# Self attention's tail in another order on TensorE, VectorE and ScalarE, and a routed unit's wait put later

## The chip, the cores and the metric

One Trainium2 chip, one core of it. The metric is the device time of one execution in microseconds (us), as the median of several runs. TensorE does matrix products and transposes into PSUM (eight banks), VectorE and ScalarE read PSUM and write SBUF, GpSimd works from SBUF to SBUF, and the SyncE queue issues most transfers. Engines run on their own and meet at semaphores.

## The reference

One layer: cross attention, self attention and a mixture of experts, each added to x. 1024 tokens of 256 numbers, in float32; what matters here is self attention's end and the experts.

```python
def _L0_attn_ref(x, Wq, Wk, Wv, Wo):          # 16 sequences of 64, 16 heads of 16
    q, k, v = ...                              # x @ Wq, x @ Wk, x @ Wv, by heads
    scores = jnp.einsum('bthd,bshd->bhts', q, k)
    scores = scores * mask                     # lower triangle; the rest becomes 0
    attn = jax.nn.softmax(scores / T ** 0.5, axis=-1)
    return jnp.einsum('bhts,bshd->bthd', attn, v).reshape(B, T, H * Dh) @ Wo

def _L0_ffn_ref(x, w_router, wg, wu, wd, sg, su, sd):   # 8 experts, 2 per token, 2 shared
    scores = jax.nn.sigmoid(logits)
    topk_w, topk_i = jax.lax.top_k(scores, TOPK)
    topk_w = topk_w / jnp.sum(topk_w, axis=-1, keepdims=True)
    ...                                        # silu(x wg) * (x wu), times wd, weighted
    out = out + jnp.einsum('tji,jhi->th', sgate * sup, sd)   # the shared experts

x = x + _L0_xattn_ref(_layernorm(x), ctx_2048, ...)
x = x + _L0_attn_ref(_layernorm(x), ...)
x = x + _L0_ffn_ref(_layernorm(x), ...)
```

## The kernel before

The tokens are worked in eight tiles of 128 (NT = 8). Each engine has its own program, written out in order; there is no scheduler, so the order of the code is the order of the work, and semaphores (`wait_ge`, `then_inc`) tie the engines together. An instruction that waits holds up everything behind it on its engine.

Self attention takes a tile through these steps: TensorE's scores into PSUM banks 0 and 1 (`b_scores`); VectorE masks them and takes each row's maximum (`b_maximum`, lines 672 and 676); GpSimd subtracts it (`b_subtract`, line 528); ScalarE takes the exponential (`b_exp`, line 1233); TensorE transposes the probabilities into banks 4 and 5 (`b_probs_T`); ScalarE copies them to SBUF (line 1241); TensorE multiplies by the values into banks 6 and 7 (`b_values`, line 1681); VectorE divides by the sums (`b_divide`, lines 829 and 835); TensorE transposes the result into bank 2 (`b_transposes`), ScalarE copies it (`b_OT_out`, line 1227), TensorE projects it (`b_project`, line 1689), and VectorE adds it to x and takes the mean and variance (`b_residual`, lines 573 to 578). The loop over tiles keeps three tiles in flight. The code around the change is what stands behind that loop: the last steps of tiles 5, 6 and 7 (NT - 3, NT - 2, NT - 1), mixed with the first steps of the experts.

These are: GpSimd's reciprocal root of the variance (`c_rstd`, line 532), VectorE's normalized rows in pairs of tiles (`c_norms`, line 870, into `xn3`, a part of `x_up`), TensorE's transposes of such a pair (`c_transposes(g)`, four of them into bank `CT_BANK[g]`), ScalarE's copy into `xT_all` (`c_xT_out`, line 1257), and the first shared expert's products over pairs of tiles: `shared_up(m)` (line 1725, into bank `UP_BANK[m]`: 0, 1, 3, 2 and on), ScalarE's silu (`gated`, line 1262), VectorE's product (`product`, line 880) and `shared_down` (line 1737). The router's products (`logits`, line 1757) need all eight tiles transposed. All transposes have line 1320. Line 1725's groups of eight in the trace are one `shared_up`: each float32 product counts twice.

Then 20 routed units run, each of 64 rows of one expert and 64 of another. `pair_a(u)` and `pair_b(u)` (line 1817) multiply the unit's transposed rows `xnT` by the gate and up weights into banks 0, 2 and 1, 3; `hidden_T(u)` transposes the hidden rows into banks 4 and 5; `pair_down(u)` (line 1841) multiplies by the down weights into bank 6. ScalarE copies a unit's rows in `routed_x` (line 1294); it must have the products of the unit ahead behind it, since there is one `xnT`. The shared expert's last sum of the first part (group 4, bank 5) is added to x by `shared_out` (line 973), which raises `added`. Second experts' rows come by transfers of 1280 KB (line 433).

Where a wait stands matters in a plain way: `pe.wait_ge(s, n)` stops TensorE until semaphore `s` has reached `n`.

Of the kernel before, what the change touches and what calls it, by code (L numbers as in the profile page):

```python
# [25 lines left out]
NT = T // P  # L26
# [24 lines left out]
MF = GF * IC  # L51
MN = len(PAIRS) * IC
UP_BANK = [(0, 1, 3, 2)[m % 4] for m in range(MF)] + [(7, 0, 2)[m % 3] for m in range(MN - MF)]
CT_BANK = (1, 3, 6, 7)
Y_BANK = [(5, 5), (4, 4), (5, 5), (4, 4), (5, 5), (1, 1), (3, 3), (4, 5)]


# [35 lines left out]
def build(nc, dram):  # L93
    with ExitStack() as ctx:
# [468 lines left out]
        def _(dve):  # L563
# [114 lines left out]
            def b_maximum(i):  # L678
                dve.wait_ge(bs_ps, i + 1)
                after(dve, bp_done, i)  # L680
                b_masked().then_inc(bs_used, 1)
                dve.wait_ge(bs_used, i + 1)
                b_top().then_inc(bmax, 1)
# [156 lines left out]
            def b_residual(i, link_, b=5):  # L840
                dve.wait_ge(bproj_ps, i + 1)
                join(i, link_, b, x3_done)
# [37 lines left out]
                dve.tensor_tensor(hidT_ring[m % 4], sil_ring[m % 2], ps[:, UP_BANK[m], D:2 * D], ALU.mult).then_inc(up_hid, 1)  # L880

            b_residual(NT - 4, link)
            b_maximum(NT - 1)
            c_norms(0, 2, 1)
            b_divide(NT - 2, link)
            b_residual(NT - 3, link, 3)
            c_norms(2, 4, 1)
            b_divide(NT - 1, link)
            product(0)
            b_residual(NT - 2, link)  # L890
            c_norms(4, 6, 2)
            product(1)
            b_residual(NT - 1, link)
# [138 lines left out]
        def _(act):  # L1032
# [5 lines left out]
            def two(b):  # L1038
                return ps[:, b:b + 2, :].rearrange("p b (h t) -> p (b h) t", t=P)
# [190 lines left out]
            def b_exp(i):  # L1230
                act.wait_ge(bsub, i + 1)

                act.activation(pr[:], sc[:], ACT.Exp, scale=SSCALE).then_inc(bp_done, 1)

            def b_step(i, parity, ahead, next_, behind):
                if ahead:
                    b_xT_out(i + 2)
                if behind:
                    b_OT_out(i - 1)
                act.wait_ge(bpt_ps, i + 1)  # L1240
                act.copy(prT, two(4)).then_inc(bpt_done, 1)
                if ahead:
                    b_k_out(i + 2)
                if next_:
                    b_exp(i + 1)
                if ahead:
                    b_v_out(i + 2, parity)
# [15 lines left out]

            act.wait_ge(absorb_m, 4)
            act.wait_ge(zeroed, 16 * ZC)
            b_step(NT - 2, 0, False, True, True)
            c_xT_out(0)
            b_step(NT - 1, 1, False, False, True)
            gated(0)
            gated(1)  # L1270
# [47 lines left out]
        def _(pe):  # L1318
# [449 lines left out]
            pe.wait_ge(bs_used, NT)  # L1768
            c_transposes(0)
            b_transposes(None, NT - 2)  # L1770
            b_probs_T(NT - 1)
            pe.wait_ge(ws_in, 16)
            pe.wait_ge(c_xT, 1)
            shared_up(0)
            b_values(NT - 1, 1)
            b_project(NT - 2)
            shared_up(1)
            b_transposes(None, NT - 1)
            pe.wait_ge(x3_done, NT - 2)
            c_transposes(1)  # L1780
            pe.wait_ge(x3_done, NT - 1)
            b_project(NT - 1)
            c_transposes(2)
            pe.wait_ge(c_xT, 2)
            shared_up(2)
            c_transposes(3)
            pe.wait_ge(bot_done, NT)
            shared_up(3)
            pe.wait_ge(x3_done, NT)
            shared_down(0)  # L1790
            pe.wait_ge(moe_in, 16)
# [76 lines left out]
            ahead = pair_a(0, now, True)  # L1868
            slots_T(1)
            pair_b(0, now)  # L1870
            pe.wait_ge(added, GF)

            for u in range(NU - 1):
                pe.wait_ge(uxT, u + 2)
                pe.wait_ge(b_up_in[(u + 1) % 2], 16 * ((u + 1) // 2 + 1))
                later = pair_a(u + 1, ahead, u + 2 < NU)
                hidden_T(u)
                pair_b(u + 1, ahead)
                if u + 2 < NU:
                    slots_T(u + 2)  # L1880
                pair_down(u, now)
                now, ahead = ahead, later
# [100 lines left out]
```

## Time and profile before

| | |
|---|---|
| median of 3 runs | 513.69 us (513.13 to 515.97) |
| the profiled execution | 514.32 us |
| its span | 512.5 us |
| TensorE busy | 496.6 us, 97% of the span |
| VectorE, ScalarE, GpSimd busy | 247.4, 185.1, 67.6 us |
| the chain that ended last | TensorE 87%, VectorE 6%, issue 3% |
| granted TensorE clock | 1.0 throughout |
| self attention's tail | 229.6 to 252.5 us of the span |
| first routed unit | from 312.0 us |

A row of the trace gives the start, the length, the engine, the line, the operation and the tiles. "x8" is the count of instructions merged into the row. A bracket at the end says how long the engine had been idle before it and whose end released it. A group's length is counted to the modelled end of its last product, so the next group starts a little before the row ahead of it ends. `w_routed` is the name of a large store, in parts of which self attention keeps its scores, probabilities and results until the experts' weights are loaded there; `x_up` holds the normalized rows.

### The profile page before, as it was taken

The page shows a single profiled execution, that of the slowest core. Times are in us where ns is not written, and L with a number is a line of the kernel's source. Part 1 is how long each engine was busy: PE and PEld are TensorE (multiplying, and loading weights), DVE is VectorE, ACT ScalarE, POOL GpSimd, SP SyncE. Part 2 cuts the span into 40 slices and gives each one's busy share as a digit, 9 for nine tenths or more (in the row PEclk, how much of TensorE's full clock was granted, in tenths as well). Part 3 has the DMA queues.
Part 4 walks back from the last instruction along what each step waited for, and adds up shares of the span by engine and source line. Part 5 has one row for each costly group of instructions (what it writes and reads, how often), then busy time and mean ns, then how long its engine had stood idle before and what let it go on. Part 6 is the DMA issues. An engine that isn't in the chain of part 4 may idle for free.

```text
span 512.5 us, 10574 instructions
## 1 busy us (share of the span) xinstructions
PE 496.6 (97%) x3878; PEld 361.1 (70%) x3878; DVE 247.4 (48%) x547; ACT 185.1 (36%) x533; POOL 67.6 (13%) x74
## 2 busy tenths in 40 slices
PE   8799999999999999998999998999999999999997
PEld 7566876876887788886788885555555555556886
DVE  2585776776776678888552221212212222222334
ACT  2267566666667544444411111212212112111110
POOL 6200000000000122232006500000000000000650
PEclk9999999999999999999999999999999999999999
DMA  7830000002990019300704272687877878852341
GB/s 224 300 113 22 0 22 20 0 20 82 369 388 2 2 62 428 128 0 1 277 35 133 73 263 60 262 299 258 313 278 268 321 265 280 306 198 83 86 120 41
DMA packets 24887, 82.05 MB, mean 160 GB/s; under 512 B 2928, under 2 KB 16560, under 8 KB 20880
## 3 DMA queue, kind: packets, MB, share of 16 engines
q1 hardware_dynamic: 21824, 73.30, 39.6%
q0 software_dynamic: 1536, 4.20, 2.6%
q10 hardware_dynamic: 1488, 4.00, 2.1%
q8 instruction: 28, 0.46, 0.3%
q14 instruction: 11, 0.09, 0.1%
HBM read 73.10 MB, written 8.39 MB: 159 GB/s over the span
## 4 chain that ended last, share of the span: by engine, by line
PE 87%; DVE 6%; issue 3%; DMA 1%; ACT 1%; SPq 0%; POOL 0%; DVEq 0%; POOLq 0%
PE ps L1817 17%; PE ps L1725 13%; PE ps L1320 12%; PE ps L1841 9%; PE ps L1737 6%; PE ps L1399 5%; PE ps L1349 5%; PE ps L1368 5%; PE ps L1491 3%; PE ps L1387 3%; DMA w_shared<-in_w_uqk 1%; PE ps L1341 1%; PE ps L1501 1%; PE ps L1681 1%; PE ps L1364 1%
## 5 line engine op out<-in xcount | busy, mean ns | idle before, releaser
L1817 PE MATMUL ps<-w_routed,xnT 128*64 x320 | 93.8, 436 | 1.6 <-DVE x_sb L973 1.6
L1725 PE MATMUL ps<-xT_all,w_shared 128*128 128x256 f32 x320 | 75.6, 380 | 0.0
L1817 PEld LDWEIGHTS ps<-w_routed,xnT 128*64 128x64 f32 x320 | 42.0, 137 | 38.4 <-issue 27.2
L1725 PEld LDWEIGHTS ps<-xT_all,w_shared 128*128 128x128 f32 x320 | 60.3, 190 | 8.4 <-issue 0.4
L1097 ACT ACTIVATE w_routed<-ps,neg_top 128x128 f32<-128x128 f32 x128 | 45.1, 379 | 15.9 <-DVE neg_top L648 15.9
L1841 PE MATMUL ps<-w_routed,hidT 128*64 x200 | 47.4, 384 | 0.0
L1817 PE MATMUL ps<-w_shared,xnT 128*64 128x384 f32 (+1 forms) x160 | 46.9, 436 | 0.0
L1817 PE MATMUL ps<-x_up,xnT 128*64 128x384 f32 (+1 forms) x160 | 46.9, 436 | 0.0
L1320 PEld LDWEIGHTS ps<-consts_a,w_routed 128*128 128x128 f32 x336 | 37.2, 141 | 13.5 <-issue 10.4
L1289 ACT COPY hidT<-ps 128x384 f32<-128x384 f32 x20 | 9.6, 479 | 100.7 <-PE ps L1320 100.7
L1262 ACT ACTIVATE sil<-ps 128x256 f32<-128x256 f32 x40 | 15.4, 384 | 84.3 <-PE ps L1725 84.2
L1320 PE MATMUL ps<-consts_a,w_routed 128*128 128x128 f32 x336 | 44.3, 276 | 1.1 <-DVE w_routed L835 0.5
L1841 PEld LDWEIGHTS ps<-w_routed,hidT 128*64 128x64 f32 x200 | 25.8, 137 | 15.0 <-issue 3.3
L1368 PEld LDWEIGHTS ps<-hid,w_routed 128*128 128x128 f32 x256 | 33.6, 192 | 1.2
L967 DVE COPY hidT<-ps 128x256 f32<-128x256 f32 x20 | 8.5, 425 | 53.4 <-PE ps L1320 53.4
L1368 PE MATMUL ps<-hid,w_routed 128*128 128x128 f32 x256 | 33.7, 275 | 0.0
L558 POOL DMA_INDIRECT x_up<-y_slots,slot_i x8 | 8.0, 997 | 182.7 <-DVE hidT L880 180.5
L648 DVE TENSOR_REDUCE neg_top<-ps 128x4 f32<-128x512 f32 x32 | 22.0, 689 | 16.6 <-PE ps L1368 16.1
L497 POOL TENSOR_TENSOR rstd<-mv,half 128x1 f32 (+1 forms) x16 | 9.1, 567 | 156.8 <-DVE mv L578 95.9
L1349 PE MATMUL ps<-w_routed 96*128 96x512 f32 x64 | 28.9, 593 | 0.3 <-issue 0.3
L1399 PE MATMUL ps<-w_routed 128*128 128x256 f32 x128 | 28.9, 379 | 0.0
L1097 ACT ACTIVATION_READ_ACCUMULATOR w_routed<-ps,neg_top 128x1 f32 x128 | 27.9, 218 | 0.0
(180 smaller groups left out, 873.8 us busy)
## 6 DMA issues: line engine op xcount, KB each, us to landing
w_routed<-in_w_routed SPq DMA_DIRECT2D x8, 1920.0 KB, 14.2
x_up<-in_w_routed SPq DMA_DIRECT2D x10, 1280.0 KB, 5.8
w_shared<-in_w_routed SPq DMA_DIRECT2D x10, 1280.0 KB, 6.1
b_down<-in_w_routed SPq DMA_DIRECT2D x10, 640.0 KB, 5.6
w_shared<-in_w_routed SPq DMA_DIRECT2D x10, 640.0 KB, 5.1
w_shared<-in_w_shared SPq DMA_DIRECT2D x1, 3840.0 KB, 11.8
w_shared<-in_w_uvo ACTq DMA_DIRECT2D x1, 2560.0 KB, 12.7
x_slots<-sil SPq DMA_DIRECT2D x16, 160.0 KB, 2.2
```

Source lines behind the costliest of these rows:

```text
L648: dve.tensor_reduce(neg_top[:, b, n], s[:, n], AX.X, ALU.min).then_inc(top_ready, 1)
L1097: last = act.activation(Pb[:, b, n, :], s[:, n, :], ACT.Exp, scale=-1.0, bias=neg_top[:, b, n:n + 1], accum_out=sums[:, b, n:n + 1])
L1262: act.activation(sil_ring[m % 2], ps[:, UP_BANK[m], 0:D], ACT.Silu).then_inc(up_sil, 1)
L1320: return pe.transpose(out, src, ident[:])
L1349: last = pe.matmul(ps[:, 2 * part + c, :], qcT[:], w[:, c * 512:(c + 1) * 512], start=True, stop=True)
L1368: last = pe.matmul(at[:, n * P:(n + 1) * P], QT[:, b, h:h + 2, :], KTb[:, b, :], start=False, stop=n == 3)
L1387: last = pe.matmul(ps[KVC * h:KVC * h + KVC, 4 + 2 * b, :].rearrange("p (j t) -> p j t", t=P), kv_ext[:, b, 0:KVC], PT[:, b].rearrange("p ...
L1399: last = pe.matmul(ps[:, b, 0:D], UT[:, j, h, :], w_m[:, 2 * j + h, :], start=j == h == 0, stop=j == NP_ // 2 - 1 and h == 1)
L1725: last = pe.matmul(ps[:, UP_BANK[m], half_ * D:(half_ + 1) * D].rearrange("p (n t) -> p n t", n=2), w_shared[:, j, at:at + P], xT_all[:, i ...
L1737: last = pe.matmul(ps[:, Y_BANK[g][n], n * D:(n + 1) * D], hidT_ring[m % 4][:, n * P:(n + 1) * P], w_shared[:, PAIRS[g][0], GU + c * D:GU ...
L1817: last = pe.matmul(ps[rows, b, 0:hi - lo], xnT[:, k, rows], w, start=k == 0, stop=k == KT - 1)
L1841: last = pe.matmul(ps[rows, 6, 0:D], hidT[:, c, rows], w, start=c == 0, stop=c == IC - 1)
```

## The change

Nothing of the computation is changed. The change moves steps in the code of three engines:

- VectorE: the first pair of normalizations (`c_norms(0, 2, 1)`) stands before the maxima of the last tile. The residual of tile 6 reads bank 3.
- ScalarE: the copy of the first transposed pair stands before the last tile's exponential.
- TensorE: the first shared product stands before the transposes of tile 7's probabilities; tile 6's projection goes to bank 3 and stands before tile 7's values; the fourth shared product stands before the fourth group of transposes; the waits on `x3_done` move with what they guard. The second group of transposes goes to bank 4, which held the probabilities.
- TensorE: the wait for `added` stands before unit 0's `hidden_T` instead of before unit 1's `pair_a`.

```diff
--- before.py
+++ after.py
@@ -51,7 +51,7 @@
 MF = GF * IC
 MN = len(PAIRS) * IC
 UP_BANK = [(0, 1, 3, 2)[m % 4] for m in range(MF)] + [(7, 0, 2)[m % 3] for m in range(MN - MF)]
-CT_BANK = (1, 3, 6, 7)
+CT_BANK = (1, 4, 6, 7)
 Y_BANK = [(5, 5), (4, 4), (5, 5), (4, 4), (5, 5), (1, 1), (3, 3), (4, 5)]
 
 
@@ -880,14 +880,14 @@
                 dve.tensor_tensor(hidT_ring[m % 4], sil_ring[m % 2], ps[:, UP_BANK[m], D:2 * D], ALU.mult).then_inc(up_hid, 1)
 
             b_residual(NT - 4, link)
+            c_norms(0, 2, 1)
             b_maximum(NT - 1)
-            c_norms(0, 2, 1)
             b_divide(NT - 2, link)
             b_residual(NT - 3, link, 3)
             c_norms(2, 4, 1)
             b_divide(NT - 1, link)
             product(0)
-            b_residual(NT - 2, link)
+            b_residual(NT - 2, link, 3)
             c_norms(4, 6, 2)
             product(1)
             b_residual(NT - 1, link)
@@ -1232,13 +1232,16 @@
 
                 act.activation(pr[:], sc[:], ACT.Exp, scale=SSCALE).then_inc(bp_done, 1)
 
+            def b_prT_out(i):
+                act.wait_ge(bpt_ps, i + 1)
+                act.copy(prT, two(4)).then_inc(bpt_done, 1)
+
             def b_step(i, parity, ahead, next_, behind):
                 if ahead:
                     b_xT_out(i + 2)
                 if behind:
                     b_OT_out(i - 1)
-                act.wait_ge(bpt_ps, i + 1)
-                act.copy(prT, two(4)).then_inc(bpt_done, 1)
+                b_prT_out(i)
                 if ahead:
                     b_k_out(i + 2)
                 if next_:
@@ -1263,8 +1266,10 @@
 
             act.wait_ge(absorb_m, 4)
             act.wait_ge(zeroed, 16 * ZC)
-            b_step(NT - 2, 0, False, True, True)
+            b_OT_out(NT - 3)
+            b_prT_out(NT - 2)
             c_xT_out(0)
+            b_exp(NT - 1)
             b_step(NT - 1, 1, False, False, True)
             gated(0)
             gated(1)
@@ -1768,24 +1773,24 @@
             pe.wait_ge(bs_used, NT)
             c_transposes(0)
             b_transposes(None, NT - 2)
-            b_probs_T(NT - 1)
             pe.wait_ge(ws_in, 16)
             pe.wait_ge(c_xT, 1)
             shared_up(0)
+            b_probs_T(NT - 1)
+            pe.wait_ge(x3_done, NT - 2)
+            b_project(NT - 2, 3)
             b_values(NT - 1, 1)
-            b_project(NT - 2)
             shared_up(1)
             b_transposes(None, NT - 1)
-            pe.wait_ge(x3_done, NT - 2)
             c_transposes(1)
-            pe.wait_ge(x3_done, NT - 1)
             b_project(NT - 1)
             c_transposes(2)
             pe.wait_ge(c_xT, 2)
+            pe.wait_ge(x3_done, NT - 1)
             shared_up(2)
-            c_transposes(3)
             pe.wait_ge(bot_done, NT)
             shared_up(3)
+            c_transposes(3)
             pe.wait_ge(x3_done, NT)
             shared_down(0)
             pe.wait_ge(moe_in, 16)
@@ -1868,12 +1873,13 @@
             ahead = pair_a(0, now, True)
             slots_T(1)
             pair_b(0, now)
-            pe.wait_ge(added, GF)
 
             for u in range(NU - 1):
                 pe.wait_ge(uxT, u + 2)
                 pe.wait_ge(b_up_in[(u + 1) % 2], 16 * ((u + 1) // 2 + 1))
                 later = pair_a(u + 1, ahead, u + 2 < NU)
+                if u == 0:
+                    pe.wait_ge(added, GF)
                 hidden_T(u)
                 pair_b(u + 1, ahead)
                 if u + 2 < NU:
```

TensorE's order in self attention's tail, before. `x_up` in a transpose is a normalized pair, `w_routed` with `bon` a divided result, `w_routed` with `bp_done` the probabilities.

```order
L1320 MATMUL ps<-consts_a,x_up 128x128 [waits c_xn3,bs_used]
L1320 MATMUL ps<-consts_a,x_up 128x128 x3
L1320 MATMUL ps<-consts_a,w_routed 128x128 [waits bon]
L1320 MATMUL ps<-consts_a,w_routed 128x128
L1320 MATMUL ps<-consts_a,w_routed 128x128 [waits x3_done,bp_done]
L1320 MATMUL ps<-consts_a,w_routed 128x128 x7
L1725 MATMUL ps<-xT_all,w_shared 128x256 [waits c_xT,ws_in]
L1725 MATMUL ps<-xT_all,w_shared 128x256 x3
L1681 MATMUL ps<-w_routed,xT_all 64x66 [waits bv_done,bpt_done]
L1681 MATMUL ps<-w_routed,xT_all 64x66 x15
L1689 MATMUL ps<-w_routed 128x256 [waits bot_done]
L1689 MATMUL ps<-w_routed 128x256
```

The same place now (all lines are five higher):

```order
L1325 MATMUL ps<-consts_a,x_up 128x128 [waits c_xn3,bs_used]
L1325 MATMUL ps<-consts_a,x_up 128x128 x3
L1325 MATMUL ps<-consts_a,w_routed 128x128 [waits bon]
L1325 MATMUL ps<-consts_a,w_routed 128x128
L1730 MATMUL ps<-xT_all,w_shared 128x256 [waits c_xT,ws_in]
L1730 MATMUL ps<-xT_all,w_shared 128x256 x3
L1325 MATMUL ps<-consts_a,w_routed 128x128 [waits x3_done,bp_done]
L1325 MATMUL ps<-consts_a,w_routed 128x128 x7
L1694 MATMUL ps<-w_routed 128x256 [waits bot_done,x3_done]
L1694 MATMUL ps<-w_routed 128x256
L1686 MATMUL ps<-w_routed,xT_all 64x66 [waits bv_done,bpt_done]
L1686 MATMUL ps<-w_routed,xT_all 64x66 x15
```

The shared product moved ahead of the probabilities' transposes, and the projection ahead of the values.

TensorE at the end of the tail, before, from the third group of transposes on:

```order
L1320 MATMUL ps<-consts_a,x_up 128x128 [waits c_xn3]
L1320 MATMUL ps<-consts_a,x_up 128x128 x3
L1725 MATMUL ps<-xT_all,w_shared 128x256 [waits c_xT]
L1725 MATMUL ps<-xT_all,w_shared 128x256 x3
L1320 MATMUL ps<-consts_a,x_up 128x128 [waits c_xn3]
L1320 MATMUL ps<-consts_a,x_up 128x128 x3
L1725 MATMUL ps<-xT_all,w_shared 128x256 [waits bot_done]
L1725 MATMUL ps<-xT_all,w_shared 128x256 x3
```

The same place now:

```order
L1325 MATMUL ps<-consts_a,x_up 128x128 [waits c_xn3]
L1325 MATMUL ps<-consts_a,x_up 128x128 x3
L1730 MATMUL ps<-xT_all,w_shared 128x256 [waits x3_done,c_xT]
L1730 MATMUL ps<-xT_all,w_shared 128x256 x3
L1730 MATMUL ps<-xT_all,w_shared 128x256 [waits bot_done]
L1730 MATMUL ps<-xT_all,w_shared 128x256 x3
L1325 MATMUL ps<-consts_a,x_up 128x128 [waits c_xn3]
L1325 MATMUL ps<-consts_a,x_up 128x128 x3
```

Both shared products now stand ahead of the last group of transposes.

VectorE in the tail, the difference (+ is now, - before):

```order
+L870 TENSOR_SCALAR x_up<-x_sb,mv,rstd 128x256 x2
 L672 TENSOR_TENSOR w_routed<-ps,consts_b 128x1024
 L676 TENSOR_REDUCE smx<-w_routed 128x16
-L870 TENSOR_SCALAR x_up<-x_sb,mv,rstd 128x256 x2
 L829 RECIPROCAL srec<-ps 128x16
```

The pair of normalizations moved from behind the last maxima to their front.

## Rows read from the trace of the kernel before

**Rows 1.** TensorE in order of time: start us, us, engine, line, operation, tiles [idle before, releaser].

```profile
232.23 1.16 PE L1681 MATMUL ps<-w_routed,xT_all 128*64 128x66 f32 x32 [0.24 <-ACT xT_all L1241]
234.97 0.63 PE L1320 MATMUL ps<-consts_a,x_up 128*128 128x128 f32 x4 [1.58 <-DVE x_up L870]
236.08 1.31 PE L1320 MATMUL ps<-consts_a,w_routed 128*128 128x128 f32 x10 [0.48 <-DVE w_routed L835]
237.22 1.89 PE L1725 MATMUL ps<-xT_all,w_shared 128*128 128x256 f32 x8
239.05 1.16 PE L1681 MATMUL ps<-w_routed,xT_all 128*64 128x66 f32 x32
...
243.82 1.10 PE L1689 MATMUL ps<-w_routed 128*128 128x256 f32 x4 [0.17 <-ACT w_routed L1227]
244.76 0.60 PE L1320 MATMUL ps<-consts_a,x_up 128*128 128x128 f32 x4
...
248.18 0.66 PE L1320 MATMUL ps<-consts_a,x_up 128*128 128x128 f32 x4 [1.10 <-DVE x_up L870]
...
252.55 1.99 PE L1725 MATMUL ps<-xT_all,w_shared 128*128 128x256 f32 x8
```

**Rows 2.** VectorE in order of time, the same stretch.

```profile
230.12 1.23 DVE L672 TENSOR_TENSOR w_routed<-ps,consts_b 128x1024 f32<-128x1024 f32 x1
231.38 1.22 DVE L676 TENSOR_REDUCE smx<-w_routed 128x16 f32<-128x1024 f32 x1
232.52 2.31 DVE L870 TENSOR_SCALAR x_up<-x_sb,mv,rstd 128x256 f32<-128x256 f32 x2
234.75 0.25 DVE L829 RECIPROCAL srec<-ps 128x16 f32<-128x16 f32 x1
...
237.60 0.73 DVE L870 TENSOR_SCALAR x_up<-x_sb,mv,rstd 128x256 f32<-128x256 f32 x2
240.25 0.26 DVE L829 RECIPROCAL srec<-ps 128x16 f32<-128x16 f32 x1 [1.93 <-PE ps L1681]
...
243.45 0.73 DVE L870 TENSOR_SCALAR x_up<-x_sb,mv,rstd 128x256 f32<-128x256 f32 x2
...
247.40 0.73 DVE L870 TENSOR_SCALAR x_up<-x_sb,mv,rstd 128x256 f32<-128x256 f32 x2 [0.81 <-POOL rstd L532]
```

**Rows 3.** VectorE in order of time, a narrower stretch.

```profile
232.84 1.99 DVE L870 TENSOR_SCALAR x_up<-x_sb,mv,rstd 128x256 f32<-128x256 f32 x1
```

**Rows 4.** GpSimd in order of time: the subtraction of the first and last tile.

```profile
176.02 1.90 POOL L528 TENSOR_TENSOR w_routed<-w_routed,smx 128x1024 f32<-128x1024 f32 x1 [3.53 <-DVE smx L676]
...
232.68 2.00 POOL L528 TENSOR_TENSOR w_routed<-w_routed,smx 128x1024 f32<-128x1024 f32 x1 [4.61 <-DVE smx L676]
```

**Rows 5.** VectorE in order of time, beside the first tile's subtraction.

```profile
175.85 1.65 DVE L663 TENSOR_SCALAR w_routed<-ps,consts_b 128x256 f32<-128x256 f32 x4
177.42 0.65 DVE L598 TENSOR_SCALAR xn<-x_sb,mv,rstd 128x256 f32<-128x256 f32 x1
```

**Rows 6.** ScalarE in order of time, self attention's tail.

```profile
231.17 1.01 ACT L1241 COPY xT_all<-ps 128x1024 f32<-128x1024 f32 x1 [0.60 <-PE ps L1320]
234.71 1.06 ACT L1233 ACTIVATE w_routed<-w_routed 128x1024 f32<-128x1024 f32 x1 [2.53 <-POOL w_routed L528]
...
243.31 0.37 ACT L1227 COPY w_routed<-ps 128x256 f32<-128x256 f32 x1
```

**Rows 7.** TensorE in order of time, the first routed units.

```profile
318.62 0.53 PE L1817 MATMUL ps<-w_routed,xnT 128*64 x1 [1.62 <-DVE x_sb L973]
...
326.51 0.49 PE L1817 MATMUL ps<-w_routed,xnT 128*64 x1
```

**Rows 8.** ScalarE in order of time, the first routed units.

```profile
317.33 0.37 ACT L1294 COPY xnT<-ps 128x256 f32<-128x256 f32 x1
```

**Rows 9.** VectorE in order of time, the first routed units.

```profile
317.80 0.68 DVE L973 TENSOR_TENSOR x_sb<-x_sb,ps 128x512 f32<-128x512 f32 x1
```

**Rows 10.** Line 433, the loads of second experts' rows: from issue to landing.

```profile
DMA to landing us min/median/max: 5.7/6.0/8.4
```

## The prediction

> **What bounds the kernel now.** I read TensorE's order of time first, then that of the engines it waits for. In self attention's tail [rows 1] the reader is to look at the brackets: 0.24, 1.58, 0.48, 0.17 and 1.10 us of idle time between 232 and 248.2, 3.57 us in all, and from 252.55 the shared expert's products run without a bracket. So TensorE sets the pace, and a microsecond taken out of these brackets is a microsecond of the whole, provided that the transfers and the routing that follow keep step. One more bracket stands at the first routed unit: 1.62 us at 318.62 [rows 7]. Together 5.19 us: that is all that this change can win, 1.0% of the time.
>
> The two large brackets in the tail wait for VectorE's normalizations (L870). The pair at 232.52 takes 2.31 us, while the pairs at 237.60, 243.45 and 247.40 take 0.73 us [rows 2]. Its second member alone took 1.99 us [rows 3]; it began 0.16 us after GpSimd's subtraction at 232.68 and ended 0.15 us after that one's end at 234.68 [rows 4]. The same is seen at the first tile: a normalization issued at 177.42 ended at 178.07, 0.15 us after the subtraction's end at 177.92, while four operations of VectorE that read PSUM took 1.65 us in all in the middle of that subtraction, 0.41 each [rows 4, 5]. So a normalization from SBUF to SBUF waits until GpSimd's big operation is over, and operations on PSUM don't.
>
> **The change part by part.** Times are those of the profiled execution (514.32 us, span 512.5; it lies 0.63 above the median of 513.69). I call the tiles 5, 6, 7.
>
> *Normalizations before the last maxima (VectorE).* They move from 232.52 to 230.12, where nothing of GpSimd's runs, and cost 0.73 instead of 2.31. The maxima end 0.65 to 0.73 us later: 232.60 becomes 233.3 [rows 2]. They don't delay the divide of tile 6, which needs the values' products: these end at 232.23 + 1.16 = 233.39 [rows 1]. So the divide starts at 233.43 instead of 234.75, and TensorE, which followed the divide's start by 236.08 - 234.75 = 1.33, can transpose its result at 234.76. The first group of normalized transposes needs only the values' end and starts at 233.35 instead of 234.97; TensorE then waits some 0.8 us for the divide. GpSimd's subtraction starts at 233.35 and lasts 1.9 to 2.0, and the exponential after it 1.06 [rows 4, 6]: ready at 236.4.
>
> *The order on TensorE.* Two transposes (0.25 to 0.3; ten took 1.31), the first shared product (1.83, from 237.22 to 239.05), then the probabilities' eight transposes: 234.76 + 0.29 + 1.83 = 236.88, behind the exponential by 0.5 us, so that wait is covered. They end near 237.94. The copy of the probabilities takes 1.01 plus 0.09 around it (232.18 to 232.23 on the way to TensorE) [rows 1, 6]: values of tile 7 at 239.04. Before it was 239.05. All of the 1.58 and 0.48 has been spent there, but tile 6's projection (about 0.95), which stood behind these values, now runs under the copy. It writes another bank (3), free since the residual of tile 5, which VectorE finishes near 236.3 (the pair behind that residual started 237.60 - 234.75 = 2.85 after the divide; 233.43 + 2.85) [rows 2].
>
> *What follows the values.* VectorE starts its divide at 240.25 as before, and everything behind it keeps its time: divide, product, residual, pair of normalizations, ending at 243.45 + 0.73 = 244.18 [rows 2]. TensorE now reaches the third group of transposes early: its shared product ends about 0.95 sooner, ScalarE's copy and with it the projection of tile 7 start near 242.9 instead of 243.82, over near 243.95. It waits 0.3 for the normalizations and starts at 244.23 instead of 244.76: 0.53 gained. A wait on VectorE takes the place of one on ScalarE.
>
> *Two shared products in front of the last transposes.* The bracket of 1.10 at 248.18 goes: TensorE gets there at about 244.2 + 0.4 + 2 x 1.8 = 248.2, and the last normalizations, which ended at 248.13 following the projection's end at 244.92 by 3.21, now end near 247.6 to 247.8. With 0.06 for the overlap that a wait costs (1.89 busy, 1.83 from start to start) that is 1.16. The product that stood after the wait now stands before it, with the same work. Tail: 0.53 + 1.16 = 1.69. The bounds: all of 3.57, if the waits for VectorE vanished too; nothing, if tile 7's values came 1.7 us later. I take 1.7, since each step goes by a row. The second group of transposes, now in bank 4, needs the probabilities copied out, which the values ahead of it on TensorE have waited for already.
>
> *Routed wait.* TensorE left unit 0 at 318.62 - 1.62 = 317.00. The addition it waited for ran from 317.80 to 318.48 [rows 9]; unit 1's first products don't touch its bank. But they need unit 1's transposed rows, which ScalarE copies from 317.33 to 317.70 [rows 8], and TensorE follows a releaser by 0.14 (318.48 to 318.62). So it starts at 317.84: 0.78 gained of the 1.62. The moved wait stands 2.7 us later, in front of the transposes of the hidden rows, at 320.6, and is long over. Queued behind it are only the unit's own transposes and the copies to them. Bounds: 0 and 1.62. The second expert's rows for unit 2 are requested when unit 0's products end, at a time that doesn't move, and needed 326.51 - 318.62 = 7.9 after unit 1's start: at 325.7, 8.7 after the products' end. The slowest such load took 8.4, the median 6.0 [rows 10].
>
> Moving ScalarE's copy of the first transposes ahead of the exponential costs nothing: it runs at 234.0 to 234.6, under GpSimd's subtraction.
>
> Sum: 1.69 + 0.78 = 2.5 us; 514.32 becomes 511.8, the median 513.69 becomes **511.2**.
>
> **A rule weighed.** The Trainium skill, "SBUF — State Buffer", section "Who interferes with whom", gives VectorE and GpSimd one pair of ports under an exclusive lock: a tensor_scalar in its two-port mode takes it, so does an instruction with two SBUF inputs against a GpSimd operation that reads SBUF, and the first to issue blocks the other wholly. The trace agrees on the first kind: 1.99 instead of 0.4 us. By the page the divide, which reads PSUM and one SBUF operand, would run beside the subtraction, and the sum stays. The second kind is seen by no row here; were the divide of that kind, the first rival's price would hold.
>
> **Rivals.**
> 1. *Slower: the subtraction is locked out.* It now issues within 0.1 us of VectorE's divide instead of under a blocked normalization. Should the divide or what follows keep GpSimd out, it would wait for VectorE's run of divide, residual and normalizations, which took from 234.75 to 238.33, 3.58 us: from 233.43 to 237.0. Subtraction to 238.9, exponential to 240.05, transposes at 240.1 instead of 236.88: 3.2 lost. Net 1.69 - 3.2 + 0.78 = -0.75: 514.4. It turns slower than before once the delay passes 2.5 us beyond the 0.5 that are covered. Against it: the operations on PSUM beside the first subtraction, where both kept their time [rows 4, 5]. Chance 0.04.
> 2. *The tail gives back half.* The divide, not the subtraction, is blocked until 235.3: 1.9 later, 1.69 becomes about -0.2, and 513.1 in all. Or a smaller slip of some tenths at the copy of the probabilities, where nothing is covered: 512. Chance 0.12.
> 3. *The change does little at the routed unit*: the copy on ScalarE, or unit 2's load at its slowest, leaves 0.3 of 0.78: 511.7. Chance 0.10.
> 4. *More than forecast*: tile 7's chain on VectorE runs sooner, since its product and residual find no wait, or the copies' overheads are smaller: 0.4 to 0.8 more, 510.6. Chance 0.16.
>
> **How the numbers follow.** The forecast has 0.58, its own range 510.8 to 511.7. The bound of 0.5%, about what a measurement of this kernel can tell from no change, lies at 511.12, next to the forecast: so its 0.58 splits into 0.30 same and 0.28 faster. With rival 4 (0.16) faster has 0.44. Rivals 2 and 3 are same, and so is a part of rival 1, whose 514.4 is above the median by less than 0.5%: same 0.53. Slower by over 0.5% needs a longer lockout than rival 1's: 0.03. The range, 510.3 to 513.0, takes in rivals 3, 4 and most of 2 and leaves out 1.
>
> **What would show it.** The pair of normalizations at about 230.1 takes 0.73; TensorE waits 0.8 for the divide at 234.8, about 0.1 for the copy near 239, 0.3 for the normalizations near 244.2, and nothing at the fourth group. The shared product that stood at 252.55 starts near 250.9, and the routed bracket shrinks to 0.84 with ScalarE's copy as releaser. It is wrong if an operation of VectorE beside the last subtraction exceeds its usual time, if values of tile 7 start after 239.5, or if the time between the first routed unit and the end changes.

## The result and the profile after

| | before | changed |
|---|---|---|
| median of 7 runs each | 514.62 us | 511.73 us |
| ratio, 95% interval | | 0.9939 (0.9914 to 0.9963) |
| once more, 17 and 12 runs | 514.43 us | 511.37 us |
| ratio, 95% interval | | 0.9949 (0.9929 to 0.9969) |
| the profiled execution, its span | 514.32, 512.5 us | 511.88, 510.1 us |

The forecast was 511.2 from 513.69, a ratio of 0.9952. The kernel is faster by 0.5 to 0.6%; both intervals lie below 1 and both take in 0.995, so that it is faster is clear, and on which side of the bound of 0.5% it lies is not. One of the changed kernel's first seven runs (518.27 us, granted clock 0.993) was over 1.5% above the fastest and is left out of the first ratio, though not of the median. The medians of the second row alone would give 0.9940; the ratio of 0.9949 with its interval is the recorded one. The page of the changed kernel, TensorE's busy time and the last-ending chain by engine:

```profile
PE 497.6 (98%) x3878; PEld 362.0 (71%) x3878; DVE 245.3 (48%) x547; ACT 184.7 (36%) x533; POOL 67.5 (13%) x74
...
PE 89%; DVE 4%; ACT 2%; DMA 1%; issue 1%; SPq 1%; DVEq 0%; ACTq 0%
```

TensorE's share of the chain grew from 87% to 89%, VectorE's fell from 6% to 4%. In the changed kernel the lines have moved by five or less: the copy of the probabilities is L1237 (1241 before), all transposes L1325, the values L1686, the projections L1694, the shared products L1730. TensorE in order of time, the changed kernel, to be laid beside [rows 1]:

```profile
231.22 1.03 PE L1694 MATMUL ps<-w_routed 128*128 128x256 f32 x4
232.49 1.16 PE L1686 MATMUL ps<-w_routed,xT_all 128*64 128x66 f32 x32 [0.24 <-ACT xT_all L1237]
...
235.04 0.44 PE L1325 MATMUL ps<-consts_a,w_routed 128*128 128x128 f32 x2 [0.81 <-DVE w_routed L835]
235.31 1.89 PE L1730 MATMUL ps<-xT_all,w_shared 128*128 128x256 f32 x8
237.04 1.04 PE L1325 MATMUL ps<-consts_a,w_routed 128*128 128x128 f32 x8
237.92 1.03 PE L1694 MATMUL ps<-w_routed 128*128 128x256 f32 x4
239.18 1.16 PE L1686 MATMUL ps<-w_routed,xT_all 128*64 128x66 f32 x32 [0.24 <-ACT xT_all L1237]
...
244.36 0.65 PE L1325 MATMUL ps<-consts_a,x_up 128*128 128x128 f32 x4 [0.23 <-DVE x_up L870]
244.85 3.62 PE L1730 MATMUL ps<-xT_all,w_shared 128*128 128x256 f32 x16
248.31 0.60 PE L1325 MATMUL ps<-consts_a,x_up 128*128 128x128 f32 x4
...
250.89 1.99 PE L1730 MATMUL ps<-xT_all,w_shared 128*128 128x256 f32 x8
```

Three brackets of the tail are left, 0.24, 0.81 and 0.24, and a small one of 0.23; before there were five with 3.57 us. The brackets fell by 2.05 us and the stretch got shorter by only 1.91 (below): the sum of the brackets is not the gain either, since where a wait stands changes what its bracket leaves out (last section). VectorE, GpSimd and ScalarE at the same place [rows 2, 4, 6]:

```profile
230.38 0.73 DVE L870 TENSOR_SCALAR x_up<-x_sb,mv,rstd 128x256 f32<-128x256 f32 x2
231.03 1.22 DVE L672 TENSOR_TENSOR w_routed<-ps,consts_b 128x1024 f32<-128x1024 f32 x1
...
233.70 0.26 DVE L829 RECIPROCAL srec<-ps 128x16 f32<-128x16 f32 x1 [0.19 <-PE ps L1686]
...
240.39 0.26 DVE L829 RECIPROCAL srec<-ps 128x16 f32<-128x16 f32 x1 [3.10 <-PE ps L1686]
...
246.98 0.74 DVE L870 TENSOR_SCALAR x_up<-x_sb,mv,rstd 128x256 f32<-128x256 f32 x2 [0.81 <-POOL rstd L532]
```

```profile
233.58 1.90 POOL L528 TENSOR_TENSOR w_routed<-w_routed,smx 128x1024 f32<-128x1024 f32 x1 [5.25 <-DVE smx L676]
```

```profile
235.52 1.06 ACT L1233 ACTIVATE w_routed<-w_routed 128x1024 f32<-128x1024 f32 x1 [0.66 <-POOL w_routed L528]
...
238.12 1.01 ACT L1237 COPY xT_all<-ps 128x1024 f32<-128x1024 f32 x1 [1.28 <-PE ps L1325]
```

The first pair of normalizations took 0.73 instead of 2.31 us, and the subtraction kept its 1.90 with the divide starting 0.12 us behind it. The first routed unit, TensorE, ScalarE and VectorE [rows 7 to 9]:

```profile
316.18 0.53 PE L1822 MATMUL ps<-w_routed,xnT 128*64 x1 [0.83 <-ACT xnT L1299]
```

```profile
315.67 0.37 ACT L1299 COPY xnT<-ps 128x256 f32<-128x256 f32 x1
```

```profile
316.15 0.68 DVE L973 TENSOR_TENSOR x_sb<-x_sb,ps 128x512 f32<-128x512 f32 x1
```

TensorE now starts 0.03 us after VectorE's addition begins, instead of 0.14 after its end; what it waits for is the copy, which ends at 316.04.

**Where the time went.** The start of a step differs between executions (below), so steps are compared by distances. I use two landmarks: tile 5's projection (230.97 before in that profile, 231.22 changed) and the shared product behind the router (252.55 and 250.89).

| stretch | before | changed | |
|---|---|---|---|
| start to tile 5's projection | 230.97 | 231.22 | +0.25 |
| from there to the product behind the router | 21.58 | 19.67 | -1.91 |
| from there to unit 0's first products | 59.41 | 59.42 | 0.0 |
| from there to unit 1's first products | 6.66 | 5.88 | -0.78 |
| from there to the end | 193.9 | 193.9 | 0.0 |

The sum is -2.4, the difference of the spans. Two starts of the kernel before that this table uses, tile 5's projection and unit 0's first products, then unit 0's in the changed kernel:

```profile
230.97 1.03 PE L1689 MATMUL ps<-w_routed 128*128 128x256 f32 x4
311.96 0.54 PE L1817 MATMUL ps<-w_routed,xnT 128*64 x1
```

```profile
310.30 0.54 PE L1822 MATMUL ps<-w_routed,xnT 128*64 x1
```

### The profile page after: what moved, and what is told of

Same layout as the page of the kernel before. It is cut to its first block, busy times and chain, and to the rows that moved or that the text cites. A ratio compares the mean times of both kernels' runs of the same rounds, so it can differ in the third digit from the quotient of the medians.

```text
span 510.1 us, 10574 instructions
## 1 busy us (share of the span) xinstructions
PE 497.6 (98%) x3878; PEld 362.0 (71%) x3878; DVE 245.3 (48%) x547; ACT 184.7 (36%) x533; POOL 67.5 (13%) x74
## 4 chain that ended last, share of the span: by engine, by line
PE 89%; DVE 4%; ACT 2%; DMA 1%; issue 1%; SPq 1%; DVEq 0%; ACTq 0%
PE ps L1822 18%; PE ps L1730 13%; PE ps L1325 13%; PE ps L1846 9%; PE ps L1742 6%; PE ps L1404 5%; PE ps L1373 5%; PE ps L1354 5%; PE ps L1496 3%; PE ps L1392 3%; PE ps L1686 2%; DMA w_routed<-in_ctxT 1%; ACT w_routed L1097 1%; PE ps L1506 1%; PE ps L1346 1%
## 5 line engine op out<-in xcount | busy, mean ns | idle before, releaser
L1730 PE MATMUL ps<-xT_all,w_shared 128*128 128x256 f32 x320 | 75.6, 380 | 0.0
L1730 PEld LDWEIGHTS ps<-xT_all,w_shared 128*128 128x128 f32 x320 | 60.3, 190 | 8.4 <-issue 0.4
L1325 PEld LDWEIGHTS ps<-consts_a,w_routed 128*128 128x128 f32 x336 | 38.1, 143 | 14.0 <-issue 10.4
L1325 PE MATMUL ps<-consts_a,w_routed 128*128 128x128 f32 x336 | 45.4, 280 | 1.4 <-DVE w_routed L835 0.8
```

Source lines behind the costliest of these rows:

```text
L1325: return pe.transpose(out, src, ident[:])
L1730: last = pe.matmul(ps[:, UP_BANK[m], half_ * D:(half_ + 1) * D].rearrange("p (n t) -> p n t", n=2), w_shared[:, j, at:at + P], xT_all[:, i ...
```

## The experiments

The changed kernel and the version with all three further steps ran in five rounds beside the kernel before; the others ran once each for their traces, and the one with the projection moved back twice. The figure to compare is the distance from tile 5's projection to the product behind the router (the *tail's distance*), 21.58 before and 19.67 changed, and in the second profile of the changed kernel 19.67 again (230.63 to 250.30). Distances of the same code in the tail agree within 0.02 us.

**The routed wait alone.**

```diff
 (kernel before)
             pair_b(0, now)
-            pe.wait_ge(added, GF)
...
+                if u == 0:
+                    pe.wait_ge(added, GF)
                 hidden_T(u)
```

> The kernel before with only the wait for `added` moved behind unit 1's first products. Theory (ScalarE's copy of unit 1's rows is next in line): the bracket at the first routed unit falls from 1.62 to 0.84 us with the copy as releaser, the tail before it keeps its brackets of 1.58, 0.48 and 1.10, and the span falls by 0.8 us. Rival (the bracket goes whole, or comes back at unit 2's load or at the transposes of the hidden rows): the span falls by 1.6, or by less than 0.3.

TensorE at the first routed unit:

```profile
317.64 0.53 PE L1817 MATMUL ps<-w_routed,xnT 128*64 x1 [0.83 <-ACT xnT L1294]
```

The bracket is 0.83 with ScalarE's copy as releaser; from unit 0's first products to unit 1's it is 5.87 us (311.77 to 317.64) instead of 6.66, and the tail's distance is 21.59. The two parts of the change are independent: 0.79 here, the rest in the tail.

**The normalizations alone.**

```diff
 (kernel before)
+            c_norms(0, 2, 1)
             b_maximum(NT - 1)
-            c_norms(0, 2, 1)
```

> The kernel before with only VectorE's first pair of normalizations moved ahead of the last maxima. Theory (the order on TensorE is needed to use it): the pair takes 0.73 instead of 2.31 us and the bracket of 1.58 goes, but TensorE then waits for the last tile's exponential in front of its transposes, the values of tile 7 start within 0.2 us of before, and the product behind the router starts within 0.2 us of before, counted from the values of tile 6 (20.3 us). Rival (the blocked normalization was the whole loss): that distance falls by 1.2 to 1.6 us.

TensorE in the tail, from tile 5's projection:

```profile
229.46 1.03 PE L1689 MATMUL ps<-w_routed 128*128 128x256 f32 x4
230.72 1.16 PE L1681 MATMUL ps<-w_routed,xT_all 128*64 128x66 f32 x32 [0.24 <-ACT xT_all L1241]
...
233.27 0.44 PE L1320 MATMUL ps<-consts_a,w_routed 128*128 128x128 f32 x2 [0.80 <-DVE w_routed L835]
234.86 1.09 PE L1320 MATMUL ps<-consts_a,w_routed 128*128 128x128 f32 x8 [1.15 <-ACT w_routed L1233]
...
243.32 0.60 PE L1320 MATMUL ps<-consts_a,x_up 128*128 128x128 f32 x4
...
251.11 1.99 PE L1725 MATMUL ps<-xT_all,w_shared 128*128 128x256 f32 x8
```

The tail's distance is 21.65, 0.07 more than before. The bracket of 1.58 is gone and so is most of the reason for it, but a bracket of 0.80 in front of the divided result and one of 1.15 for the exponential (releaser ACT L1233) stand in its place: 1.95 for 2.06. The loss on VectorE was real and worth nothing by itself.

**The order without the normalizations.**

```diff
 (changed kernel)
-            c_norms(0, 2, 1)
             b_maximum(NT - 1)
+            c_norms(0, 2, 1)
```

> The changed kernel with the first pair of normalizations put back behind the last maxima. Theory: the pair takes 2.3 us again, the divide of tile 6 starts 1.3 us later, the first shared product and with it everything up to tile 7's values is later by 1.3 to 1.4 us, and the product behind the router starts 19.8 us after the values of tile 6 instead of 18.4. Rival (the order on TensorE alone brings the gain): it starts within 0.3 us of 18.4.

TensorE in the same place, from tile 6's values:

```profile
230.14 1.16 PE L1686 MATMUL ps<-w_routed,xT_all 128*64 128x66 f32 x32 [0.24 <-ACT xT_all L1237]
232.89 0.63 PE L1325 MATMUL ps<-consts_a,x_up 128*128 128x128 f32 x4 [1.59 <-DVE x_up L870]
233.99 0.44 PE L1325 MATMUL ps<-consts_a,w_routed 128*128 128x128 f32 x2 [0.48 <-DVE w_routed L835]
...
243.40 0.66 PE L1325 MATMUL ps<-consts_a,x_up 128*128 128x128 f32 x4 [0.23 <-DVE x_up L870]
...
249.93 1.99 PE L1730 MATMUL ps<-xT_all,w_shared 128*128 128x256 f32 x8
```

From the values of tile 6 (230.14) to the product behind the router (249.93) are 19.79, 1.39 more than changed; expected were 19.8. The distance from tile 6's values to the third group of transposes puts the four cases of the first part side by side:

| | normalizations late | normalizations early |
|---|---|---|
| old order on TensorE | 12.53 | 12.60 |
| new order | 13.26 | 11.87 |

Over this first part each step alone loses (0.07 and 0.73), together they gain 0.66. (The new order also brings the last group's gain further on: over the whole tail this kernel has 21.05, 0.53 less than before.) In the old order the first shared product stands between the probabilities' transposes and tile 7's values and covers ScalarE's copy. In the new order it stands ahead of the transposes, and the projection covers the copy, with 0.24 of waiting. With late normalizations that puts tile 7's values 8.08 us behind tile 6's instead of 6.82, for nothing: the exponential ended at 235.09, and the transposes start only at 236.08, behind the product. With early ones the product stands where TensorE would wait for the exponential, the 1.15 of the experiment above.

**The last group of transposes.**

```diff
 (changed kernel)
             shared_up(2)
+            c_transposes(3)
             pe.wait_ge(bot_done, NT)
             shared_up(3)
-            c_transposes(3)
```

> The changed kernel with the last group of transposes put back between the third and the fourth shared product. Theory: a bracket of 1.1 to 1.2 us stands in front of that group again, and the product behind the router starts 1.2 us later than 18.4 us after the values of tile 6. Rival (VectorE is early enough by now, since the last residual came 0.4 us sooner): the bracket is under 0.8 and so is the loss.

TensorE at tile 5's projection, the last group and the product behind the router:

```profile
231.45 1.03 PE L1694 MATMUL ps<-w_routed 128*128 128x256 f32 x4
...
248.00 0.66 PE L1325 MATMUL ps<-consts_a,x_up 128*128 128x128 f32 x4 [1.02 <-DVE x_up L870]
...
252.36 1.99 PE L1730 MATMUL ps<-xT_all,w_shared 128*128 128x256 f32 x8
```

The tail's distance is 20.91: 1.24 of the 1.91 is this step, as expected; the bracket, expected at 1.1 to 1.2, shows 1.02 only. It counts from the modelled end of the product ahead, while work that finds no wait begins before that end; see the last section.

**Tile 6's projection behind tile 7's values.** This ran twice.

```diff
 (changed kernel)
+            b_values(NT - 1, 1)
             pe.wait_ge(x3_done, NT - 2)
             b_project(NT - 2, 3)
-            b_values(NT - 1, 1)
```

> The changed kernel with tile 6's projection put back behind tile 7's values. Theory (it fills the time in which ScalarE copies tile 7's probabilities): the bracket in front of these values grows from 0.24 to 1.2 us, the values start no earlier, the bracket of 0.23 in front of the third group of transposes goes, and the product behind the router starts 19.0 us after the values of tile 6 instead of 18.4. Rival (the projection's place is free, the early normalizations alone brought the first part): 18.4 within 0.15.

> The kernel with tile 6's projection behind tile 7's values once more, for the 3.40 us in the router's products in which TensorE stood with nothing to wait for. If that stop goes with where this program's instructions lie, it comes back at the same product; if it is chance of one execution, it is gone, and the product behind the router starts 20.1 us after tile 5's projection (19.7 in the changed kernel).

The second execution:

```profile
230.66 1.03 PE L1694 MATMUL ps<-w_routed 128*128 128x256 f32 x4
...
238.62 1.16 PE L1686 MATMUL ps<-w_routed,xT_all 128*64 128x66 f32 x32 [1.10 <-ACT xT_all L1237]
...
250.74 1.99 PE L1730 MATMUL ps<-xT_all,w_shared 128*128 128x256 f32 x8
```

The tail's distance is 20.08, 0.41 more than changed; I had expected 0.6 at first, and 20.1 for this second execution. The bracket in front of the values grew from 0.24 to 1.10, and they started 6.69 us after tile 6's in both kernels. So the projection is what filled the copy's time. The first execution agrees up to there (values 6.69 us after tile 6's, a bracket of 1.10); behind it came a stop that is told in the last section.

**Which operations of VectorE GpSimd's subtraction locks out.** Two operations were added between the last maxima and the divide. Their results go to an unused store.

```diff
 (changed kernel)
+            dve.bn_stats(y_sb[:, 0:6], x_sb[:, 0, :])
+            dve.tensor_tensor(y_sb[:, 16:], x_sb[:, 0, 16:], x_sb[:, 1, 16:], ALU.add)
             b_divide(NT - 2, link)
```

In the control the second line is `dve.bn_stats(y_sb[:, 6:12], x_sb[:, 1, :])`.

> The changed kernel with two more operations on VectorE between the last maxima and the divide of tile 6, whose results nobody reads: statistics over 256 numbers of one SBUF tile (0.43 us, it lets GpSimd's subtraction begin), then a sum of two SBUF tiles of 240 numbers, issued in the middle of the subtraction. If an instruction with two SBUF inputs is locked out by a GpSimd operation that reads SBUF: the sum takes 1.3 to 1.7 us and ends 0.1 to 0.2 us after the subtraction. Rival (only the two-port form is locked out): it takes 0.4 us as such sums do elsewhere.

> The control to the kernel with the sum: in its place a second statistics operation, with one SBUF input, whose result nobody reads. Both theories: it takes 0.43 us beside the subtraction and the subtraction keeps its 1.9 us. If anything of VectorE from SBUF were locked out, it would take 1.3 us or more.

VectorE with the sum, then GpSimd in the same run, then VectorE in the control:

```profile
233.33 1.99 DVE L886 TENSOR_TENSOR y_sb<-x_sb 128x240 f32<-128x240 f32 x1
235.24 0.24 DVE L829 RECIPROCAL srec<-ps 128x16 f32<-128x16 f32 x1
```

```profile
233.16 1.90 POOL L528 TENSOR_TENSOR w_routed<-w_routed,smx 128x1024 f32<-128x1024 f32 x1 [5.24 <-DVE smx L676]
```

```profile
233.33 0.41 DVE L886 BATCH_NORM_STATS2 y_sb<-x_sb 128x6 f32<-128x256 f32 x1
233.66 0.24 DVE L829 RECIPROCAL srec<-ps 128x16 f32<-128x16 f32 x1
```

The sum took 1.99 us and ended at 235.32, 0.26 after the subtraction's end at 235.06; the control's operation took 0.41, and the subtraction 1.90 in both. I had expected 1.3 to 1.7 us for the sum, ending 0.1 to 0.2 after the subtraction. Both were too low: the sum issued 0.17 us after the subtraction's start, not in its middle, and ended a little later behind it. The tail's distance is 21.61 with the sum (230.81 to 252.42) and 20.03 with the control (230.81 to 250.84). So two unhindered operations cost 0.36 more than the changed kernel's 19.67, and the same place with one of them locked out 1.94; the lockout itself costs the difference, 1.58.

**A further version.** The traces point to what still waits. The third pair of normalizations can run when the second has (its rstd is ready, and VectorE is idle for 3.10 us before the last divide). The first group of transposes can stand ahead of tile 6's values, where TensorE waits 0.24 for a copy anyway, and the first shared product then ahead of the divided result. And unit 1's transposed rows can go to a buffer of their own (`y_sb`, unused until unit 0's result), so that ScalarE copies them ahead of unit 0's second silu.

```diff
 (changed kernel)
             c_norms(2, 4, 1)
+            c_norms(4, 6, 2)
...
             b_residual(NT - 2, link, 3)
-            c_norms(4, 6, 2)
...
-            b_values(NT - 2, 0)
             pe.wait_ge(bs_used, NT)
             c_transposes(0)
-            b_transposes(None, NT - 2)
+            b_values(NT - 2, 0)
             pe.wait_ge(ws_in, 16)
             pe.wait_ge(c_xT, 1)
             shared_up(0)
+            b_transposes(None, NT - 2)
...
-            unit(0)
-            routed_x(1)
+            unit(0, first_x)     # first_x, between the two silus: unit 1's rows into y_sb
```

> The changed kernel with three more steps: the third pair of normalizations right behind the second, since its rstd is ready by 237.6; the first group of transposes ahead of tile 6's values and the first shared product ahead of the transposes of tile 6's result; and unit 1's transposed rows copied to another buffer ahead of unit 0's second silu. Theory: the bracket in front of the third group goes, tile 7's values start about 0.4 us sooner, held then by the last exponential, and the product behind the router starts 17.8 us after the project step of tile 5 would have let tile 6's values start (18.4 now); the bracket at the first routed unit goes whole (0.84). Together 1.4 us. Rival (VectorE's divide, later by 0.27 behind the values, decides the tail): the tail gains under 0.2 and only the routed unit's 0.84 is left.

> The kernel with three further steps but without the first group of transposes moved ahead of tile 6's values: that group stands where the changed kernel has it. Theory (that step alone brings tile 7's values forward by 0.4 to 0.5): from tile 5's projection to the product behind the router 19.3 to 19.4 us, since only the bracket of 0.23 in front of the third group goes; the routed unit's bracket is gone. Rival (the early third pair of normalizations brings it all): 18.9 as with all three.

> The changed kernel once more, timed in five rounds beside the kernel before. Theory: 0.9950 of before, within 0.9930 to 0.9970, and from tile 5's projection to the product behind the router 19.7 us against 21.6. Rival (part of the first measurement was chance): the ratio is 0.997 or above.

> The changed kernel with the three further steps (third pair of normalizations early, first group of transposes ahead of tile 6's values, unit 1's rows in a buffer of their own), timed in five rounds beside the kernel before. Theory: 1.6 us less than the changed kernel by the trace, so 0.9918 of before. Rival (gains of this size are lost in what differs from execution to execution): a ratio no lower than that of the changed kernel.

TensorE of the version with all three, second profile:

```profile
230.35 1.03 PE L1702 MATMUL ps<-w_routed 128*128 128x256 f32 x4
...
235.75 1.09 PE L1333 MATMUL ps<-consts_a,w_routed 128*128 128x128 f32 x8 [0.44 <-ACT w_routed L1236]
...
237.94 1.16 PE L1694 MATMUL ps<-w_routed,xT_all 128*64 128x66 f32 x32 [0.24 <-ACT xT_all L1240]
...
249.20 1.99 PE L1738 MATMUL ps<-xT_all,w_shared 128*128 128x256 f32 x8
```

| | tail's distance | bracket at the routed unit | ratio to before, 95% |
|---|---|---|---|
| before | 21.58 | 1.62 | 1 |
| changed | 19.67 | 0.83 | 0.9949 (0.9929 to 0.9969) |
| two further steps (without the first group's) | 19.21 | 0 | one execution |
| all three | 18.85 | 0 | 0.9903 (0.9875 to 0.9930) |

In these versions lines stand up to nine higher than in the changed kernel. The first execution of the version with all three has 18.85 and no routed bracket as well. All three steps gain 0.82 in the tail. Of it the early third pair has 0.46 (I expected 0.3), and the first group of transposes, together with the first shared product ahead of the divided result, 0.36 (I expected 0.4 to 0.5). What holds the tail now is the last exponential (0.44, releaser ACT L1236) and the copy of the probabilities (0.24). With the routed bracket's 0.83 that makes 1.65, where I expected 1.4.

By distances the routed part is less even. Unit 1's first products come 4.87 us after unit 0's instead of 5.88, 1.01 sooner; unit 2's first products come 7.83 us after unit 1's in one execution of the version with all three, but 8.09 in the other and 8.22 in the one with two steps (7.88 in the changed kernel). There the load of unit 2's second expert had taken 7.0 us from issue to landing, and 5.9 in the execution with 7.83. The execution with two steps shows it as a bracket:

```profile
322.23 0.53 PE L1831 MATMUL ps<-w_routed,xnT 128*64 x1 [0.22 <-issue]
```

Its load was issued at 314.94 and landed 7.0 later, 0.3 us before these products start; the profile names no releaser, so that the load is the next limit at this place is likely and not shown. Up to unit 2 the step brings 1.06, 0.80 and 0.67 us in the three executions.

The version's median was 509.10 us (509.10 / 514.43 is 0.9896, the recorded ratio 0.9903; I had expected 0.9918), the changed kernel's 511.37 beside the same runs of before. The two intervals overlap by a hair, but they share the runs of before. Directly, five of the version's six runs (507.96 to 509.64) are below all twelve of the changed kernel (510.15 to 514.90), so it is the faster of the two.

## Why the prediction was right

*Normalizations.* As said: 0.73 at 230.4, no wait for GpSimd. That a normalization is locked out by the subtraction was read from [rows 3 to 5], and with the normalizations put back the pair took 2.31 again; the run with the sum shows the same for an operation of two SBUF inputs, and its control that a statistics operation on one SBUF input is not locked out. The Trainium skill's "SBUF — State Buffer", section "Who interferes with whom", has these as separate cases (a tensor_scalar in its two-port mode, two SBUF inputs, one SBUF input outside such a mode), and the traces now agree with all three: 1.99, 1.99 and 0.41 us. The prediction called the second kind unseen and kept the sum by the divide's PSUM operand; that held, since the divide's four products took 1.00 beside the subtraction.

*Rival 1 and 2*, a lockout of the subtraction or the divide, did not happen: the subtraction started 0.08 us behind the maxima's end and took 1.90 us, and the divide ran beside it. Rival 2's price was of the right size: with the sum in front of it the divide started 1.95 us later, and the tail lost 1.94. Rival 1's case, a subtraction kept out by VectorE, was made by no run, so its price is untested; its net is -0.73 by its own terms, not -0.75.

*Tile 7's values.* I had them at the same distance as before (6.81 us after tile 6's; before 6.82). They came at 6.69. The term that was mis-sized is the first shared product, for which I took 1.83 from a row where values follow it; here the next group starts after 1.73 (235.31 to 237.04). Other rows have 1.73 or 1.83 too (1.83 from 240.27 to 242.10, where transposes follow as well), and which of the two a product gets is not explained by any run. The 0.81 in front of the divided result is as forecast (0.8). The copy's bracket is 0.24 where 0.1 was named, but the time from the probabilities' transposes to the values is as in the sum (2.14 against 2.16).

*The third group of transposes.* Predicted 0.53 sooner, measured 0.66, the same 0.13, since VectorE's chain from the divide on kept its length and began 0.12 sooner. Its bracket is 0.23 against 0.3: a wait on VectorE took the place of that on ScalarE.

*The last group.* Predicted 1.16, measured 1.26, and 1.24 when it was put back. I added 0.06 to the bracket of 1.10 for the overlap; it is 0.16: before, the product at 245.19 was followed after 2.99 us, unhindered it is 1.73.

*The routed wait.* 0.78 predicted and measured in the changed kernel, 0.79 alone, with ScalarE's copy as releaser. Unit 2's load did not show here: unit 2 starts 7.88 us after unit 1 (7.89 before), and from unit 1's products to the end the distances agree. It did show once unit 1 started another 1.01 us sooner, in the further version.

The sum was 2.47 and the trace has 2.69 in the two places. That is inside the forecast's own range (510.8 to 511.7) and short of rival 4, which asked for 0.4 to 0.8 more; the 0.22 are the two terms above, a product followed sooner and an overlap counted too small. That the product behind the router starts at 250.89, where 250.9 was forecast, is luck: the opening of that execution was 0.25 us later, which hides the difference.

## What to carry to other kernels

Before moving a stalled operation, ask what the engine behind it does next: here the freed 1.58 us turned into waits for a divide and an exponential until the consumer's order was changed too, and that order alone lost 0.73. When an engine stands at a wait, look for a later step whose inputs are ready; a wait belongs directly in front of the first instruction that needs it, and behind it the next releaser tells how much can be had. Keep VectorE's normalizations from SBUF and sums of two SBUF tiles out of GpSimd's long operations, and put there what reads PSUM, or statistics.

## What the runs showed of the hardware

*A bracket is less than the wait costs.* Before the last group the bracket is 1.10 and its removal brought 1.26; in the experiment it is 1.02 and costs 1.24. From the start of the product ahead to the start of the waiting group it is 2.99 and 2.92 us, against 1.73 without a wait: 1.26 and 1.19. The rest of the 1.24 is in the waiting group itself, which is followed after 0.49 instead of 0.44 (0.50 before). Between before and changed this last part cancels, since there the third group waits instead (0.49 instead of 0.43).

*The opening differs from execution to execution by as much as the change is worth.* In the traces of before and of the experiments tile 5's projection starts between 228.88 and 231.45 us, though no program differs ahead of it on TensorE. Totals of single runs say nothing here; distances inside a trace do, to 0.02 us in the tail; where a load sets the pace they differ too (7.83 to 8.22 us at unit 2 of the further version). The totals go with the mean granted clock: of 17 executions of before beside the last two kernels, the eight with a clock of 0.992 or 0.993 took 514.8 to 516.3 us, the four with 0.999 or 1.000 took 512.0 to 513.8. The changed kernel's twelve beside them had a mean clock of 0.9969 against 0.9955, so a part of the difference of the totals may be the clock's: all together the means differ by 2.8 us; taken at like clocks, by 1.9 (0.999 and up, 5 changed and 4 before), 2.5 (0.995 to 0.997, 5 and 5) and 1.8 (below, 2 and 8). The 2.7 from the traces don't rest on the totals.

*A stop without a releaser.* In the first execution of the kernel with the projection behind the values, TensorE stood for 3.40 us in the midst of the router's products, with nothing that the profile shows to wait for:

```profile
249.32 0.97 PE L1762 MATMUL ps<-consts_b,xT_all 128*32 128x8 f32 x95
253.70 0.62 PE L1762 MATMUL ps<-consts_b,xT_all 128*32 128x8 f32 x33 [3.40 <-issue]
254.25 3.78 PE L1730 MATMUL ps<-xT_all,w_shared 128*128 128x256 f32 x8
```

The granted clock had been 1.00; in the 3.4 us of the stop it averaged 0.93 and from 253.7 to 260.0 it was 0.50, the lower of the two levels (1.2 GHz), so that the product behind it took 3.78 instead of 1.99 us. The span is 516.3 us, and 509.9 in the second execution of the same program, which had neither the stop nor the slow stretch. The core's transfers ran at 420 GB/s during the stop (the experts' weights); they ran at 430 between 250 and 256 us before, with no stop. What caused it is open.
